# A state-space block and a spiking layer on one core: the spikes' transposes moved within their steps, and the last image's membrane added by VectorE

## What is computed

```python
# layer 0: group norm, then a selective state-space block with D = 512 channels and 16 states
xz = gn(x) @ W_in;  xh, z = split(xz)
xc = depthwise_conv3x3(xh)
dt_r, Bp, Cp = split(xc @ W_xproj)
dt  = softplus(dt_r @ W_dt + b_dt)
dtN = dt @ W_dtN + b_dtN
# over the 48*48 positions of an image, in order, for every channel and state:
h = exp(dt * A) * h + (dtN * B) * xc
y = sum_over_states(h * C) + Dskip * xc
x = x + (layernorm(y) * ln_g + ln_b) * silu(z) @ W_out + b_out

# layer 1: group norm, a dense layer, and a neuron that integrates over the images (b is its time axis)
u = gn(x) @ W.T + b
v = v + (u - v) / 2
s = (v >= 1)
v = v * (1 - s)
x = x + s
```

## Time and profile before

| | us |
|---|---|
| median of 3 runs | 4340.82 (4330.65 to 4343.32) |
| the profiled execution | 4342.65 |
| its span, first to last instruction | 4340.7 |

### The profile page before, as it was taken

One profiled execution on the slowest core, in us unless ns is written; L12 is line 12 of the kernel. 1 busy time (PEld: TensorE's weight loads), 2 busy tenths in 40 slices (PEclk: granted clock), 3 DMA queues, 4 the chain that ended last, 5 costly groups with the idle time before them and its releaser, 6 DMA issues.

```text
span 4340.7 us, 64778 instructions
## 1 busy us (share of the span) xinstructions
PE 3593.2 (83%) x20628; PEld 2275.0 (52%) x20628; DVE 3951.9 (91%) x3833; ACT 3452.2 (80%) x5878; POOL 3847.0 (89%) x2518
## 2 busy tenths in 40 slices
PE   6788888888888888888888888888888888888877
PEld 3455555555555555555555555555555555555554
DVE  3999999999999999999999999999999999999994
ACT  3788887888888888888887888888888888888874
POOL 3999999889998899988998889988899889998993
PEclk8899999999999999999999999999998999999988
DMA  5223323332233223322232223222332233223310
GB/s 132 64 80 96 85 60 92 91 101 62 77 92 101 75 62 100 95 78 71 87 99 75 75 76 99 82 75 75 107 86 64 75 102 101 65 60 100 90 42 22
DMA packets 189296, 355.05 MB, mean 82 GB/s; under 512 B 27416, under 2 KB 164120, under 8 KB 188960
## 3 DMA queue, kind: packets, MB, share of 16 engines
q1 hardware_dynamic: 188960, 350.92, 28.3%
HBM read 289.84 MB, written 61.01 MB: 81 GB/s over the span
## 4 chain that ended last, share of the span: by engine, by line
PE 27%; ACT 23%; DVE 22%; issue 17%; POOL 10%; DMA 0%; DVEq 0%; ACTq 0%; SPq 0%; POOLq 0%
DVE st L1059 17%; PE ht L1197 8%; POOL st L608 8%; ACT decay L736 6%; ACT L933 3%; PE work L1273 3%; PE work L1230 2%; DVE y L1035 2%; ACT dt L809 2%; ACT weighed L765 2%; PE work L1299 2%; PE work L1280 2%; ACT L809 2%; PE work L1170 2%; PE work L1240 2%
## 5 line engine op out<-in xcount | busy, mean ns | idle before, releaser
L1059 DVE TENSOR_TENSOR_SCAN st<-decay,st 128x1024 f32<-128x1024 f32 (+1 forms) x1536 | 2730.8, 1778 | 137.0 <-ACT decay L736 106.7
L608 POOL TENSOR_TENSOR st<-xc,bbc 128x1536 f32<-128x1536 f32 x768 | 2652.8, 3454 | 57.5 <-DMA bbc<-brow 50.9
L736 ACT ACTIVATE decay<-dt,neg_a 128x1024 f32<-128x1024 f32 (+1 forms) x1536 | 1353.7, 899 | 356.2 <-DVE st L1059 349.0
L1197 PE MATMUL ht<-ident,st 128*128 128x128 f32 x9216 | 1326.8, 294 | 291.9 <-DVE st L1059 268.4
L1197 PEld LDWEIGHTS ht<-ident,st 128*128 128x128 f32 x9216 | 1114.5, 151 | 596.3 <-DVE st L1059 448.0
L1035 DVE SCALAR_TENSOR_TENSOR y<-ht,ct,y 128x512 f32<-128x512 f32 x1536 | 1120.3, 729 | 66.1 <-PE ht L1197 64.8
L641 POOL TENSOR_TENSOR y<-y,weighed 128x512 f32<-128x512 f32 x672 | 856.5, 1275 | 278.3 <-ACT weighed L765 276.8
L765 ACT ACTIVATE weighed<-ht,ct 128x512 f32<-128x512 f32 x672 | 459.1, 683 | 230.8 <-PE ht L1197 226.7
L1170 PE MATMUL work<-tri,conv_w 96*32 96x384 f32 x4608 | 433.5, 511 | 11.6 <-DMA tri<-rows_of_xh 4.4
L1235 PE MATMUL work<-xn,win 128*128 128x384 f32 x768 | 329.5, 572 | 94.8 <-DVE volt L1015 58.6
L1230 PE MATMUL work<-xn,win 128*128 128x384 f32 (+1 forms) x768 | 297.5, 511 | 5.8 <-ACT xn L865 3.2
(11 more groups left out here) (114 smaller groups left out, 3368.0 us busy)
## 6 DMA issues: line engine op xcount, KB each, us to landing
bbc<-brow SPq DMA_DIRECT2D x192, 768.0 KB, 6.6
tri<-rows_of_xh SPq DMA_DIRECT2D x576, 200.0 KB, 4.2
rows_of_xh<-xhp SPq DMA_DIRECT2D x160, 200.0 KB, 1.9
out_dram<-ot SPq DMA_DIRECT2D x43, 384.0 KB, 3.8
xin<-in_x_dram SPq DMA_DIRECT2D x42, 384.0 KB, 3.8
rows_of_xh<-xhp SPq DMA_DIRECT2D x32, 250.0 KB, 2.1
st<-in_x_dram SPq DMA_DIRECT2D x6, 384.0 KB, 5.5
out_dram<-y SPq DMA_DIRECT2D x4, 384.0 KB, 2.5
```

What stands on the lines that cost most here:

```text
L608: u = g.tensor_tensor(slot, xc[:, kq % 2, :, :], bbc[:, piece_slot(kq, p), n % PIECE, :].unsqueeze(1).to_broadcast([P, DC, T]), ALU.mult)
L736: a.activation(flat(decay[:, :, :])[:, lo:hi], flat(dt[:, (k + ahead) % 2, :, :])[:, lo:hi], ACT.Exp, scale=neg_a[:, n:n + 1]).then_inc(s_ ...
L1059: v.tensor_tensor_scan(state[:, lo:hi], flat(decay[:, :, :])[:, lo:hi], state[:, lo:hi], 0.0 if h == 0 else state[:, lo - 1:lo], ALU.mult, ...
L1197: last = t.transpose(ht[:, m, c * P:(c + 1) * P], st[:, j, c, m * P:(m + 1) * P], ident[:, :])
```

## The change

In the main loop, `to{kc}_0` and `to{kc}_1` go from `early` to the end of `late` in their steps. Their place on TensorE and on ScalarE moves with that, and so do the turns of the banks within the step. In the last image, TensorE no longer adds the membrane with an identity matmul; VectorE adds it into the `ht` bank in place, raises a new semaphore, and waits for it before it fires.

```diff
@@ groups(k, s) @@
     for kc, a in L1_SLOTS.get(k, ()):
         dve += [(L1, f"l{kc}_{h}") for h in range(CH) if s == l1_step(a, h)]
         if s == TO_STEP[a]:
-            early += [(L1, f"to{kc}_0"), (L1, f"to{kc}_1")]
+            late += [(L1, f"to{kc}_0"), (L1, f"to{kc}_1")]
@@ semaphores @@
         s_end_l = sem("last_image_l1_filled")
+        s_end_v = sem("last_image_charged")
@@ VectorE, behind the main loop @@
             for j in range(K * CH):
                 kc, h = divmod(j, CH)
                 cols = slice(kc * T, (kc + 1) * T)
+                now = ht[:, j % NHT, 0:T]
                 dve.wait_ge(s_end_l, j + 1)
+                v.tensor_tensor(now, now, volt[:, h, cols], ALU.add).then_inc(s_end_v, 1)
                 need(dve, s_end_t, 2 * (kc - 1))
-                v.scalar_tensor_tensor(out=end_spikes(kc, h), in0=ht[:, j % NHT, 0:T], scalar=fire_at[:, h:h + 1],
+                dve.wait_ge(s_end_v, j + 1)
+                v.scalar_tensor_tensor(out=end_spikes(kc, h), in0=now, scalar=fire_at[:, h:h + 1],
                                        in1=img[:, img_par(B, -1), h, cols], op0=ALU.is_ge,
                                        op1=ALU.add).then_inc(s_end_f, 1)
@@ TensorE, end_l1(j) @@
                 need(pe, s_end_f, j - NHT + 1)
-                t.matmul(ht[:, j % NHT, 0:T], ident[:, :], volt[:, h, kc * T:(kc + 1) * T], start=True, stop=False)
                 for hi in range(CH):
                     last = t.matmul(ht[:, j % NHT, 0:T], w1s[:, hi, h * P:(h + 1) * P],
                                     img[:, img_par(B, -1), hi, kc * T:(kc + 1) * T],
-                                    start=False, stop=hi == CH - 1)
+                                    start=hi == 0, stop=hi == CH - 1)
```

## The result

The changed kernel takes 4383.61 us in the median of six runs (4376.63 to 4387.60), the kernel before 4340.00 in six beside them: a ratio of 1.0102, 95% interval 1.0090 to 1.0113. It is slower by 43.6 us, and the time lies above the predicted range. The profiled execution has a span of 4383.3 us against 4340.7, so its stretches can be compared one by one.

What follows compares the result with a forecast made beforehand. No single engine was the bound: the loop is a ring, where VectorE's scan waits for ScalarE's decay. Terms +1.5 - 6.6 + 16.8 + 4 - 7.1 = +8.6 us, on 4342.65, gave 4351 us; range 4333 to 4370.

Steps and rivals of the forecast that it cites:

- part 1, at full clock: Steps 4 to 6: step 4 gains, steps 5 and 6 lose it again; +1.5 us, bounds -6 and +6.
- part 1, clock: Step 4: half of the 13.2 us lost to low clock in twelve stretches goes; -6.6 us, bounds -13.2 and +9.9.
- late x load: Step 6: load lands in time in the median, 0, bound +1 in each of 18; as rival +27, 4369, chance 0.07.
- part 2, banks: Step 14: yi0 waits for to0's bank and delays VectorE's y-add; 21 x 0.8 = +16.8 us, bounds +10 and +20.
- part 2, clock: Step 14: TensorE idles 1.3 us before to0; four clock falls of about 1.1 us, +4, bounds 0 and +23.
- part 3: Last image: twelve half-chunks lose two TensorE identity passes each, VectorE adds instead; -7.1 us, bounds -7.4 and -5.
- the rival with the clock at both new waits: Clock falls at the new waits of part 1 and part 2: +9.9 and 11 us; sum +32, 4375; chance 0.16.
- half of the twelve: Step 4: of twelve low-clock stretches, half the cost was taken to go, -6.6 us.

Runs made afterwards that it cites:

- The single fillings: Changed kernel with idle transposes on TensorE at one wait only: ten ahead of to0 in step 13, 1.0057; or four ahead of yi0 in step 14, 1.0035.
- step 4 alone: Kernel before with only the spikes of step 4 moved to the end of their step; step 13 and last image as before; 1.0019.
- the load ahead of the store: Kernel before with step 4's spikes moved, the last image's add on VectorE, and the x load issued before the spikes' store; 1.0001.
- all waits filled: Changed kernel with idle transposes on TensorE: ten ahead of to0 (step 13), four ahead of yi0 (step 14), twelve ahead of to1 (step 4); 1.0006, 4340.51 us.
- only those of steps 13 and 14: Changed kernel with idle transposes on TensorE: ten ahead of to0 in step 13 and four ahead of yi0 in step 14; 1.0055, 4359.70 us.
- the two fastest kernels here: Kernel before with VectorE's last-image add, plus: step 4's spikes moved, load before store, twelve idle transposes before to1, 0.9959; or eighteen before to0 in step 4, 0.9964.
- step 13 alone: Kernel before with only the spikes of step 13 moved to the end of their step; step 4 and last image as before; 1.0147.

## Why the prediction was wrong

The sum put beside the changed kernel's profile, in us (the first two lines: steps 4 to 6 of 21 chunks, split by the full-clock stretches):

| term | predicted | measured |
|---|---|---|
| part 1, at full clock | +1.5 | +2.9 |
| part 1, clock | -6.6 | -13.2 |
| late x load | 0 | +1.4 |
| part 2, banks | +16.8 | +22.0 |
| part 2, clock | +4 | +25.7, and +5.0 in step 0 |
| part 3 | -7.1 | -9.0 (alone: 77.9 - 70.6 = -7.3) |
| step 9 | not seen | +9.6 |

**The step that failed** is part 2's clock term: "a fall costs about 1.1: I take four, +4". It was 19 falls at 1.35 us each, and TensorE's lateness went on into step 0 (in images 1 to 6 it takes 5.87 behind a stretch at low clock, and 5.58, as before, behind the one at full clock). That is 27 of the 34 us between the forecast for this execution, 4351.3, and its time of 4385.3, beyond the bound of +23, and over twice the 11 that the rival with the clock at both new waits set for it. That rival had the sign and this place right, but it also wanted +9.9 in step 4, where the clock gave back 13.2. The first wait was foreseen rightly: 1.3 us predicted, 1.05 to 1.52 measured in the changed kernel. What I left out stood in my own working: yi0's start 0.58 us behind the end of to0's transposes is a second idle stretch of TensorE. I priced it as a delay for VectorE and not as something that the clock sees. The single fillings show that this second wait is needed: without it, no fall in 21. So is the first. And the reason given against that rival, that each new wait is shorter than the 2.31 us which felled only twelve of 21, weighed each wait by itself; two shorter ones close together felled more.

**Part 2, banks.** The mechanism held in every link: to0 starts 0.73 us after the step (foreseen 0.73), yi0 waits for `ot`, the y-add waits over 1 us. Only the size was off, 1.05 for 0.78, and the sum of 22.0 lies past the bound of +20. yi0 starts 1.40 behind to0 (938.43 to 939.83) and not 1.24, mostly since it starts 0.65 behind the start of to0's eviction (939.18) and not 0.53 (1371.06 to 1371.59 in the prediction): half of the pair's 1.02 was too little for four of the six blocks. And the states start 1.00 behind yi0 (939.83 to 940.83) and not 0.89 as before, where yi0's weight loads ran 0.32 ahead of its matmuls, as they don't at 939.83. The rows of before for that:

```profile
1370.49 1.18 PEld L1280 LDWEIGHTS work<-skip_diag,xc 128*128 128x128 f32 x8
...
1371.70 1.47 PE L1197 MATMUL ht<-ident,st 128*128 128x128 f32 x12
```

**Part 1.** Right at full clock: 4.67 + 5.00 + 5.73 = 15.40 in images 1 to 6 against 5.21 + 4.68 + 5.32 = 15.21 before, +0.19 for the predicted +0.13; 0.21 won in image 7 for 0.27. The working even holds the 5.73 of step 6 (15.34 - 9.62 = 5.72), without any late load; the expectations for step 4 alone and for the load ahead of the store, which put it down to the load, overlooked that. The clock did better than "half of the twelve", with one fall left. Alone, the move kept seven, near the half that I took; so this term's size in the changed kernel isn't explained by step 4. What the prediction says of the cause is too short: the row with the 2.31 us of idle time is from a stretch at clock 1.00, and the same wait stands ahead of all 21 stretches, of which twelve fell. It is needed (filled, it leaves the clock at 1.00 in all 21), but it doesn't settle by itself where the clock falls. The load was late nine times by the waits view, but only four stretches of step 6 grew by it (5.89 to 6.38 instead of 5.73).

**Part 3.** Right when it stands alone, -7.3 for -7.1. The -9.0 in the changed kernel lies past the bound of -7.4, and what adds the rest isn't known. Two half-chunks of the tail, the changed kernel's timeline:

```profile
4374.65 2.75 PE L1340 MATMUL ht<-img,w1s 128*128 128x384 f32 x8
...
4376.14 0.57 DVE L1142 TENSOR_TENSOR ht<-ht,volt 128x384 f32<-128x384 f32 x1 [0.66 <-PE ht L1340]
4376.81 0.62 DVE L1145 SCALAR_TENSOR_TENSOR xb<-ht,fire_at,img 128x384 f32<-128x384 f32 x1
...
4377.43 0.57 DVE L1142 TENSOR_TENSOR ht<-ht,volt 128x384 f32<-128x384 f32 x1
```

The add takes 0.57 us where 0.62 was put in. The Trainium skill's formula (VectorE: DVE Perf Modes, "The TRN2 errata") made it 0.56; the trace agrees, although one operand and the result lie in PSUM here.

**Step 9** was in no part of the working: its stretches have more of the low clock (TensorE busy 8.22 us each instead of 7.47), though nothing of the change stands there. With all waits filled its sum is 189.21, near the 190.69 of before; with only those of steps 13 and 14 it was 194.64. What sets it wasn't settled, nor why step 5 has one, two, six, seven, ten or eleven falls in kernels whose steps 4 and 5 have the same orders and the same wait of 1.50 us ahead of to1.

## What to carry to other kernels

When a move makes an engine with a gated clock wait, count every wait that it adds, the short ones behind a bank's turn too, and price them together: here the second, 0.5 us long, turned a delay of 22 us into 48. A wait that is moved rather than removed can take the low clock with it to the next step, so a gain that consists of clock is to be counted only if the idle time is gone; and idle transposes into a free buffer are a cheap way to test that, and were in the two fastest kernels here (0.9959 and 0.9964). Turns of a shared pair of buffers make a chain: a group moved later makes the next owner late, and the one repair of that which was tried, yi0 behind the states, moved the loss a step on.

## What the runs showed of the hardware

- Two waits of TensorE, of 1.05 to 1.52 and mostly 0.5 us, with 0.91 us of work between them, made the granted clock fall (0.79 in the mean of the stretch) in 19 of 21 places (16 with step 13 alone); with only the first left, or only the second, 0.6 us then, it fell in none of 21. The Trainium skill (TensorE: Matmul & The Clock Gate, "A second HAM failure mode: psum-queue depth-cycling") tells of a kernel whose TensorE idles briefly and often between groups that cycle through PSUM banks, so that the clock goes back and forth. The trace agrees, with banks that are emptied 0.5 to 1.2 us too late.
- The low clock can't be read off one step. The same instructions with the same 1.50 us wait in steps 4 and 5 had it in one to eleven of 21 places, in kernels that differ elsewhere; how much of that is the difference and how much is one execution against another isn't shown. The effects of the parts of the change didn't add up (1.53% against 1.02%).
- A fall cost 1.35 us in step 14, between 1.1 and 1.7 in step 5 (6.09 to 6.67 against 5.00), and between 2.3 and 2.8 in the three falls of step 6 (8.07, 8.11 and 8.54 against 5.73).
